# POOL's gather loop of a relational graph layer: the wait for a slot and the next gather ahead of the one-hot of the tile two back

## What is computed

```python
h = jnp.maximum(_layernorm(x, axis=-1), 0.0)
# _rgcn(h, ...):
msgs = h[src]
u = h @ root + bias
for r in range(8):
    mask = (edge_type == r).astype(h.dtype)
    sums = segment_sum(msgs * mask[:, None], dst, num_segments=n)
    cnt = segment_sum(mask, dst, num_segments=n)
    mean = sums / jnp.maximum(cnt, 1.0)[:, None]
    u = u + mean @ weight[r]
z = concatenate([u, h], axis=1) @ w_gate + b_gate
out = x + jnp.tanh(u) * z + h * (1.0 - z)
```

## Time and profile before

| | |
|---|---|
| median of 3 runs | 1606.29 us (1605.07 to 1615.55) |
| the profiled execution | 1619.65 us, of which the span of the trace is 1617.9 us |
| PE busy | 1303.7 us (81%) |
| DVE / POOL / ACT busy | 992.7 / 884.7 / 447.7 us |
| mean granted clock of TensorE | 0.919 |
| chain that ended last | POOL 27%, DMA 25%, PE 18%, issue 13%, DVE 10% |

### The profile page before, as it was taken

One profiled execution on the slowest core, in us unless ns is written; L12 is line 12 of the kernel. 1 busy time (PEld: TensorE's weight loads), 2 busy tenths in 40 slices (PEclk: granted clock), 3 DMA queues, 4 the chain that ended last, 5 costly groups with the idle time before them and its releaser, 6 DMA issues.

```text
span 1617.9 us, 20012 instructions
## 1 busy us (share of the span) xinstructions
PE 1303.7 (81%) x6045; PEld 648.0 (40%) x6045; DVE 992.7 (61%) x1276; ACT 447.7 (28%) x592; POOL 884.7 (55%) x1060
## 2 busy tenths in 40 slices
PE   3879666489998996289889889988989877668697
PEld 1434222134443443044444444444444444334364
DVE  6664488787765753265566545646647655645676
ACT  5353322533233432131322222223304122213000
POOL 2258837544887778566476657654745565531000
PEclk9989887799999998599999999989999989779899
DMA  5641002113424233167757565657688566653876
GB/s 192 205 144 49 12 33 91 64 57 93 136 84 117 64 112 84 25 198 228 228 163 234 195 194 175 212 178 221 208 259 250 150 213 195 204 176 108 214 209 183
DMA packets 125024, 248.89 MB, mean 154 GB/s; under 512 B 20246, under 2 KB 60749, under 8 KB 124940
## 3 DMA queue, kind: packets, MB, share of 16 engines
q1 hardware_dynamic: 92124, 165.39, 32.2%
q0 software_dynamic: 32816, 82.39, 18.3%
HBM read 189.22 MB, written 77.05 MB: 165 GB/s over the span
## 4 chain that ended last, share of the span: by engine, by line
POOL 27%; DMA 25%; PE 18%; issue 13%; DVE 10%; ACT 4%; SPq 2%; POOLq 1%; DVEq 0%; ACTq 0%
DMA early<-y_rows,idx 19%; POOL table_rows L608 14%; PE ps L1292 13%; PE ps L1253 4%; DMA out_dram<-hT 3%; DVE W L923 2%; POOL onehot L645 2%; POOL early L582 2%; ACT early L752 2%; POOL early L637 1%; DMA early<-u_rows 1%; DVE early L994 1%; DMA hT<-u_rows 1%; POOL dcol L626 1%; POOL idx L627 1%
## 5 line engine op out<-in xcount | busy, mean ns | idle before, releaser
L1292 PE MATMUL ps<-W,hT 128*128 128x512 f16 (+1 forms) x4740 | 1084.1, 390 | 113.7 <-DVE W L923 63.6
L1292 PEld LDWEIGHTS ps<-W,hT 128*128 128x128 f16 (+1 forms) x4740 | 487.9, 104 | 670.4 <-issue 104.8
L1253 PE MATMUL ps<-early,onehot 128*125 x768 | 212.6, 413 | 110.3 <-POOL onehot L645 69.6
L637 POOL DMA_INDIRECT early<-y_rows,idx x192 | 230.1, 1198 | 92.9 <-PE ps L1256 41.2
L608 POOL DMA_INDIRECT table_rows<-edge_src,early x160 | 226.0, 1412 | 82.3 <-issue 82.3
L645 POOL TENSOR_SCALAR onehot<-iota_d,dcol 128x125 f16<-128x125 f16 x186 | 151.5, 815 | 207.4 <-DMA early<-y_rows,idx 202.0
L777 ACT ACTIVATE yhl<-W 128x512 f16<-128x512 f32 x140 | 87.5, 627 | 510.1 <-DVE W L1048 315.0
L923 DVE SCALAR_TENSOR_TENSOR W<-W,wsc 128x2048 f16<-128x2048 f32 x71 | 176.6, 2491 | 40.6 <-ACT W L714 37.9
L1253 PEld LDWEIGHTS ps<-early,onehot 128*125 x768 | 105.3, 144 | 177.6 <-issue 137.1
L714 ACT ACTIVATE W<-W,wsc 128x2048 f16<-128x2048 f32 x71 | 140.1, 1989 | 49.5 <-DVE W L939 31.2
L1023 DVE TENSOR_TENSOR yhl<-W,yhl 128x512 f16<-128x512 f32 x140 | 114.1, 815 | 14.2 <-ACT yhl L777 13.8
(11 more groups left out here) (170 smaller groups left out, 827.5 us busy)
## 6 DMA issues: line engine op xcount, KB each, us to landing
y_rows<-yhl SPq DMA_DIRECT2D x144, 256.0 KB
W<-in_L_gnn_weight_dram SPq DMA_DIRECT2D x32, 1024.0 KB
early<-u_rows SPq DMA_DIRECT2D x30, 448.0 KB
u_rows<-early SPq DMA_DIRECT2D x30, 448.0 KB
W<-in_L_gnn_w_gate_dram SPq DMA_DIRECT2D x8, 1024.0 KB
early<-in_x_dram SPq DMA_DIRECT2D x9, 512.0 KB, 4.3
hs_rows<-early SPq DMA_DIRECT2D x9, 512.0 KB, 3.0
u_rows<-yhl SPq DMA_DIRECT2D x18, 256.0 KB
```

Of the source, the lines that this page charges most:

```text
L637: pool.indirect_dma_start(out=G[:, b, :], out_offset=None, in_=y_rows[i], in_offset=bass.IndirectOffsetOnAxis(ap=idx[:, b, :], axis=0), bo ...
L1253: nc.tensor.matmul(ps[0:DT, 4 + half, :], hot_t, rows[:, bass.ds(ring_slot * (2 * D) + (part * D + half * HC), HC)], start=first and part ...
L1292: last = nc.tensor.matmul(ps[0:rows, n % 4, :], hT[:, m, v_h, k, n0:n0 + rows], Wh[:, MAT[w][c], v_w, k, :], start=(first and v_h + v_w == ...
```

## The change

In the loop of `turn` and in that of `first_turn` the two calls change places. No instruction is added, removed or altered.

```diff
                 for b in range(2, RING):
+                    gather(i, q, b)
                     make_onehot(i, q, b - 2)
-                    gather(i, q, b)
 
             def turn(i, q):
                 for b in range(RING):
+                    gather(i, q, b)
                     make_onehot(i, q - 1 if b < 2 else q, (b - 2) % RING)
-                    gather(i, q, b)
```

## The result

| | before | changed |
|---|---|---|
| median | 1610.92 us (1605.07 to 1616.33, 4 runs) | 1648.50 us (1646.45 to 1648.75, 4 runs) |
| ratio | | 1.0231 (95% interval 1.0184 to 1.0278) |
| span of the profiled execution | 1617.9 us | 1647.0 us |

The change costs 2.3%, about 37 us. The forecast was 12 us longer, and the time lies above its range, which ended at 1643 us. The direction was right; the size was three times too small. The two spans differ by 29.1 us and not by 37, since the profiled execution of the kernel before (1619.65 us) lies 9 us above that kernel's median.

What follows compares the result with a forecast made beforehand. The prediction took PE's waits for one-hots, 77.3 us or 4.8% of the time, as what feeding could give. It summed 57 us gained and 69 paid to 12 us longer, 1618 us, range 1592 to 1643.

Steps and rivals of the forecast that it cites:

- Where the wait is: In the loop, PE stands still for tiles, never for products; feeding can give at most 77.3 us.
- The one-hot behind the slot wait: At a full ring, third or later tiles of a group wait: 32 times 2.15 us, 69 us lost.
- The link of 0.89 us: At a full ring, from the slot's freeing to the gather's start, taken as POOL's waking: 0.89 us.
- The gain: In the loop, a third gather in flight cuts PE's 77.3 us of tile waits to 20, gaining 57 us.
- the small moves: POOL's copies wait for the instruction just ahead: 0.13 us a turn, 25 us in all, covered by slack.
- the slack between groups: POOL's spare time between PE's groups of tiles, 4 us, said to cover its longer turns.
- the remainder of 20: PE's waits for one-hots left despite the third gather, from overrunning POOL instructions: 20 us, between 0 and 45.
- The slower rival: In the loop, three gathers delay one another and landings come later: 37 us longer, 1643 us; chance 0.25.
- the faster rival: In the loop, the third gather wins, as few third tiles meet a full ring: 1575 us; chance 0.15.
- The 6.3 us: In the loop, a gather's time from issue to its one-hot, read from the timeline as its flight: 6.3 us.

Runs made afterwards that it cites:

- e1: Changed kernel with the column copies of tile t+1 moved from ahead of the gather of t to behind it; ratio 1.0159 to the kernel before.
- e8: Changed order with a ring of five slots in place of four; ratio 0.9686 to the kernel before.
- e4: Kernel before with only the slot wait moved ahead of the one-hot, the gather staying behind it; ratio 1.0036 to the kernel before.
- e2: Kernel before with one number altered: the copies wait for the one-hot just ahead, not the one before it; ratio 1.0227 to the kernel before.
- e10: Kernel of e8 with the copies' wait made to ask for the one-hot just ahead; ratio 0.9887 to the kernel before.
- e7: Kernel before, its order kept, with a ring of five slots in place of four; ratio 0.9971 to the kernel before.

## Why the prediction missed the size

**Where the wait is: right.** In the loop PE never waited for a product, waits for tiles bound what feeding can give, and with a third gather in flight POOL's waits for landings went away (202.0 to 8.9 us). POOL waited for a slot in 47 places, where over 50 were forecast.

**The one-hot behind the slot wait: right price, wrong count, and a sum that is near by chance.** 32 tiles at 2.15 us, 69 us, were forecast; measured are 59.0 us in 28 places, 2.11 us in the mean. That mean is made of different things. 8 of the 28 waits are 1.97 to 2.12 us long, the full ring as it was priced; in e1, 11 are 2.18 to 2.25. 7 are 2.4 to 3.8 us, the same with a gather or one-hot that overran. 10 are 1.80 to 1.87 us: their group's second tile had waited too, and the gather ahead of their one-hot hadn't waited for a slot, so the ring wasn't full there; POOL was a turn behind. 3 are under 1.2 us. So about 15 places pay the term and not 32. The two groups of four didn't make a fourth tile wait. The mechanism stands: e8 gives the one-hots a slot more and the waits are gone. The link of 0.89 us was read as POOL's waking; by the chain above, and by the 0.19 us of e4, it is the lead of the gather.

**The gain: this step failed.** The prediction let the third gather take 57 us off PE's 77.3 and leave 20. The 20 should be what is left at first and second tiles; measured are 42.2 us there, and before it was 43.7. Next to nothing was gained. Of the 22 us that were missed, about 10 go with the small moves, which were put at nothing, and 12 stay without them (e1).

**The small moves: this step failed too.** The prediction took the new wait for the instruction just ahead at 0.13 us a turn, from one row of a tensor operation that waits for another, and let it lie in the slack between groups. It is 0.71 us: 0.23 as the copy starts 0.18 us behind the one-hot and not 0.05 ahead of its end, and 0.48 between the copy at 627 and the gather. The row that I took as the price had nothing behind the wait but one more operation. Here POOL's register instructions and semaphore waits at lines 627 to 636 stand behind it, and then the gather's lead. In the old order they ran under the one-hot; with the drain they start when it is over. In the changed kernel's trace the gathers with that gap start, in the median, 0.75 us behind the register instruction of line 636, and those that waited for a slot 0.74 us behind it. The changed kernel's timeline has the counter-example in itself, a turn whose copy took long:

```profile
926.49 0.65 POOL L645 TENSOR_SCALAR onehot<-iota_d,dcol 128x125 f16<-128x125 f16 x1
927.30 2.23 POOL L626 COPY dcol<-edge_dst 128x1 f32 x1 [0.17 <-POOL onehot L645]
929.48 0.17 POOL L627 COPY idx<-edge_src 128x1 int32 x1
929.81 1.08 POOL L637 DMA_INDIRECT early<-y_rows,idx  x1 [0.15 <-issue]
```

Under the long copy the same instructions and the lead were over in time, and the gap is 0.15 us and not 0.64. So the lead behind line 636 makes up most of the gap; what POOL does in it the trace doesn't say. That the wait for the instruction just ahead makes the gap is shown by e2 and e10, which add nothing else, and by e1, which removes it. The Trainium skill ("GPSIMD Engine Reference", section "2.1 Instruction dispatch") says that completion holds back only what waits on the instruction's semaphore, and not the next Pool instruction. By that rule the old order's copy may overlap the one-hot, and the new one's may not, and the rows at 1338.63 and 910.16 agree.

**And the slack did not cover it.** Between groups there was time on the average, but tiles come in bursts of two and three. Where PE has caught up with POOL, each next tile waits a turn less its own matmuls: 2.86 - 1.05 = 1.81 us, where it would be 1.10. That is also where the 10 third tiles at 1.8 us come from.

The other part of the error is the remainder of 20 itself. Without the drain 31.8 us stay at first and second tiles (e1), so it was 12 too low even with the small moves at no price. What makes those 12 stays open. By luck the error of 22 was partly made up, as third tiles wait 10 us less than the 69 of the sum.

**What the sum left out: the products.** It priced PE's waits and nothing of what they do to PE's clock. The changed kernel's products take 7.4 us more in the loop. The table's last two columns go roughly together: 61 us at the lower clock with 1077 us of products in e8, 143 us with 1096 in e2. They don't do so strictly (e7 has 96 and 1090.7, the kernel before 99 and 1084.1), and one kernel differs as much between two executions: the changed one has 113 and 1096.3, then 130 and 1103.4, at the same waits. So the 7.4 us are about what two executions of one kernel differ by. A kernel whose PE waits much more for tiles also has more time at the lower clock. The runs show that the two go together, and none varied the one without the other; that the waits are the cause is not shown.

Put together, on the profiled executions: the span grew by 29.1 us, of which about 27 lie in the loop. There PE waits 23.1 us more for one-hots (100.1 + 0.3 against 77.3; 12 forecast) and is 7.4 us longer at products (0 forecast), and some 3 us come back: its waits for DVE are 3.9 us shorter. The slower rival had the price right, 37 us, for the wrong cause: landings are not what PE waited for.

One number of the range is off: half way from 1606 to the faster rival's 1575 is 1591 and not 1592. Nothing hangs on it.

**The figure for a transfer.** From the figure of the Trainium skill ("DMA: Bandwidth & Descriptors", section "Anatomy of one DMA"), 2.0 us plus bytes over 436e3 per us, the prediction estimated 3.0 us for a gather, and from that, that two in flight would be enough. This case's traces say otherwise: with two in flight the median from issue to landing is 5.1 us (e7), and by e8 against e7 the third in flight is worth 2.9% of the time, where it has a slot. The 6.3 us that the prediction took from the earlier trace rows were a flight longer than most.

## What to carry to other kernels

In a ring, count two things apart: how many transfers fly while the engine waits for a landing, and how many tiles stand ready while it waits for a slot. Moving a consumer step behind a producer's wait takes from the second to give to the first; with another slot both could be had, and here it paid only then. Ask too what stands between the wait and the step: here the step behind the wait alone cost tenths of a microsecond, and two with a transfer's issue between them.

Look at every wait of an in-order engine for how far back the instruction is that it asks for. One turn back it cost nothing here; when a reordering makes it the instruction just ahead, the register and wait instructions behind it and the lead of the next transfer lose their cover, and the price is theirs and not that of the wait. Price it from a turn of the same loop with the drain put in, if you can, and not from a bare pair of operations.

When a mean agrees with what was worked out, look at the single waits before calling it confirmed. Two of the means here (2.11 and 1.13 us) agreed by chance.

## What was not expected of the hardware

- A POOL wait for the instruction just ahead, with two copies, register instructions and two more waits between it and the next indirect DMA, made a turn 2.86 us in place of 2.15, in each of the three kernels that had it (changed, e2, e10), and cost 2.3% and 2.0% of the time where it was put in alone (e2, e10). Taking it out of the changed kernel gave back 0.7%, which the intervals don't tell from nothing.
- POOL's gather begins 0.88 us after the end of the matmul that frees its slot, to the hundredth in 46 of the 47 places of the changed kernel and in 11 of the 12 before. A one-hot that waits for the same slot begins after 0.2 to 0.3 us (e4, 31 of 32 places). Most of the difference lies in the 0.74 us between the register instruction of line 636 and the gather.
- A change of waits came with a larger change of time: e8 has 45.8 us less of idle time ahead of the tiles' matmuls than the kernel before (64.5 against 110.3), and besides its products take 7.0 us less and the tiles' matmuls 7.2 us less (205.4 against 212.6, with three tiles more); its mean granted clock is 0.928 where it was 0.919.
